# Third table parts on two halves of TensorE's rows, and stores of two rows each

## The reference

```
x_slice = take_along_axis(xf, DIMS[tile_idx])            # 16 of 1024 channels
u  = clip((x_slice - mn[tile]) / (mx[tile] - mn[tile] + 1e-8), 0, 1 - 1e-6)
gi = clip(int(u * 16), 0, 15);  x_local = (u - gi/16) * 16
delta = (spline_bases[tile, j, gi] + spline_slopes[tile, j, gi] * x_local) * output_scale[tile]
out = layernorm(x + (x + scatter(delta)))                # over 1024 channels
```

## Time and profile before

| what | value |
|---|---|
| time of the runs | 1272.38 us, median of 3 (1271.8 to 1273.63) |
| the profiled execution | 1269.53 us, its span 1267.8 us |
| start of the last stage | 1119 us |
| busy share of the span | PE 89%, DVE 86%, ACT 74%, POOL 65% |
| mean TensorE clock granted | 0.92; 0.5 of full speed throughout the last stage |
| read from DRAM, written | 69.06 MB, 101.04 MB |

### The profile page before, as it was taken

The page is one execution under the profiler, slowest core; times in us unless marked ns, Lnnn a source line. Parts: engine busy times, 40 slices in busy tenths (PEclk is TensorE's granted clock), DMA queues, the critical chain, the costliest instruction groups (busy, mean ns, idle before and its releaser), DMA issues. The chain is left out here.

```text
span 1267.8 us, 31481 instructions
## 1 busy us (share of the span) xinstructions
PE 1131.2 (89%) x9273; PEld 720.2 (57%) x9278; DVE 1085.1 (86%) x2538; ACT 943.7 (74%) x1805; POOL 818.3 (65%) x1647
## 2 busy tenths in 40 slices
PE   5799999999999999999999999999999996747620
PEld 4556666666666666666666666666666663511100
DVE  4888889898989898989898999989998978887873
ACT  4657888888888888888888888888888873524771
POOL 3125666676767676767676767676767666525565
PEclk9999999999999999999999999999999998755555
DMA  4112332322222222232222222222222223859998
GB/s 145 34 39 105 107 107 107 106 105 105 105 105 105 105 105 105 105 105 105 105 105 104 104 104 104 103 101 89 102 100 102 103 73 131 348 209 366 407 419 333
DMA packets 63474, 174.88 MB, mean 138 GB/s; under 512 B 11259, under 2 KB 22467, under 8 KB 63430
## 3 DMA queue, kind: packets, MB, share of 16 engines
q1 hardware_dynamic: 52118, 149.33, 31.8%
q10 hardware_dynamic: 5808, 23.07, 4.5%
q0 software_dynamic: 5504, 1.94, 1.1%
HBM read 69.06 MB, written 101.04 MB: 134 GB/s over the span
## 5 line engine op out<-in xcount | busy, mean ns | idle before, releaser
L1189 DVE SCALAR_TENSOR_TENSOR acc<-xT_all,cw_sb,acc 128x256 f32<-128x256 f32 x768 | 354.0, 520 | 6.5 <-ACT acc L848 6.5
L875 ACT ACTIVATE sg<-TS,bet,gam 128x256 f16<-128x256 f32 x244 | 123.6, 557 | 26.6 <-PE TS L493 26.4
L513 PE MATMUL PR<-xT_all,w_sb 128*128 128x256 f32 x512 | 138.7, 395 | 2.7 <-ACT xT_all L811 2.7
L525 PE MATMUL WKB<-w_sb,tS 128*128 128x512 f32 x256 | 137.3, 618 | 0.0
L848 ACT ACTIVATE acc<-xT_all,cb_sb,cw_sb 128x256 f32<-128x256 f32 x256 | 132.5, 592 | 4.2 <-DVE xT_all L1175 2.2
L595 PE MATMUL PR<-shT,w_mg_sb 128*64 128x128 f32 x2048 | 127.8, 278 | 6.5 <-ACT shT L857 6.5
L368 POOL TENSOR_TENSOR AT<-AT,Wm 128x128 f32<-128x128 f32 x210 | 108.3, 516 | 39.2 <-DVE AT L1215 24.4
L567 PE MATMUL OB<-th_all,AT 128*128 128x512 f32 x256 | 122.7, 602 | 5.9 <-DVE AT L368 2.0
L595 PE MATMUL PR<-shT,w_rk_sb 128*64 128x128 f32 x2048 | 125.9, 276 | 0.0
L595 PEld LDWEIGHTS PR<-shT,w_rk_sb 128*64 128x64 f32 x2048 | 110.5, 137 | 25.7 <-issue 25.7
L595 PEld LDWEIGHTS PR<-shT,w_mg_sb 128*64 128x64 f32 x2048 | 112.5, 138 | 18.9 <-issue 12.0
(11 more groups left out here) (274 smaller groups left out, 2773.8 us busy)
## 6 DMA issues: line engine op xcount, KB each, us to landing
xin_all<-in_x SPq DMA_DIRECT2D x32, 1024.0 KB
y_ring<-y_all SPq DMA_DIRECT2D x32, 1024.0 KB, 4.1
y_scratch<-y_all SPq DMA_DIRECT2D x32, 1024.0 KB, 6.1
own<-y_scratch SPq DMA_DIRECT2D x5, 2048.0 KB, 17.2
rows<-y_scratch SPq DMA_DIRECT2D x4, 2048.0 KB, 12.6
out<-rows ACTq DMA_DIRECT2D x4, 2048.0 KB, 18.6
out<-own ACTq DMA_DIRECT2D x3, 2048.0 KB, 20.5
RX<-RE SPq DMA_DIRECT2D x128, 32.2 KB
```

Source lines behind the costliest of these rows:

```text
L513: i = pe.matmul(PR[:, 0:T], w0_sb[:, blk, :], xT[b][:, blk, HIST:HIST + T], start=(blk == 0), stop=(blk == NB - 1))
L525: pe.matmul(WK[h][:], tS[b][:, chunk_cols(c)], w1_sb[:, half_cols(h)], start=True, stop=False)
L875: nc.scalar.activation(sg[:, blk, :], at[:, (blk % 2) * T:(blk % 2 + 1) * T], ACT.Sign, scale=gam[:, blk:blk + 1], bias=bet[:, blk:blk + 1 ...
L1189: v.scalar_tensor_tensor(acc[:, blk, :], xT[b][:, blk, i:i + T], cw_sb[:, blk, i:i + 1], acc[:, blk, :], ALU.mult, ALU.add).then_inc(e_con ...
```

## The change

Two edits. First, `t2s2` gets 128 partitions: the table part three stands in both halves. For a pair of columns the two 128-row matmuls come first, then the third part of column 0 on rows 0 to 63, and that of column 1 on rows 64 to 127. Second, in units 0 to 10 ScalarE issues a store after each two columns, with 1 MB, in place of one of 2 MB after four; the waits on p_st count 32 for such a unit.

```diff
-        t2s2 = sbw("t2s2", [NT, TC], BF16)
+        t2s2 = sbw("t2s2", [P, TC], BF16)
...
-                    link(v.tensor_copy(t2s2[:], t2i[0:NT, :]))
+                    link(v.tensor_copy(t2s2[:], t2i[:]))
...
+            def written(u):
+
+                return sum(32 if w < DIRECT else 16 for w in range(u % NS, u + 1, NS))
+
...
                 for u in range(NS, U - 1):
-                    sp.wait_ge(p_st[slot_id(u)], stored(u - NS))
+                    sp.wait_ge(p_st[slot_id(u)], written(u - NS))
                     load(u)
...
-                    pool.wait_ge(p_st[slot_id(u)], stored(u))
+                    pool.wait_ge(p_st[slot_id(u)], written(u))
...
                     pe.wait_ge(p_zf, s - 2)
+                    cols = [slice(j * HALF, (j + 1) * HALF) for j in range(2)]
                     for j in range(2):
-                        cols = slice(j * HALF, (j + 1) * HALF)
-                        pe.matmul(Z[s % 3][:, cols], ohT[:, 2 * s + j, :], t2s01[:], start=True, stop=False)
-                        i = pe.matmul(Z[s % 3][:, cols], ohT[0:NT, 2 * s + j, :], t2s2[:], start=False, stop=True)
+                        pe.matmul(Z[s % 3][:, cols[j]], ohT[:, 2 * s + j, :], t2s01[:], start=True, stop=False)
+                    for j in range(2):
+                        rows = slice(j * NT, (j + 1) * NT)
+                        i = pe.matmul(Z[s % 3][:, cols[j]], ohT[rows, 2 * s + j, :], t2s2[rows, :], start=False, stop=True)
                     i.then_inc(z_rd, 1)
...
-                        if u < DIRECT and n % 4 == 3:
+                        if u < DIRECT and n % 2 == 1:
+                            pair = slice(n % 4 - 1, n % 4 + 1)
                             act.wait_ge(p_row, n + 1)
-                            nc.scalar.dma_start(out_u[u], slot(u)).then_inc(p_st[slot_id(u)], 16)
+                            nc.scalar.dma_start(out_u[u][:, pair, :], slot(u)[:, pair, :]).then_inc(p_st[slot_id(u)], 16)
```

More of the change, by code:

```diff
@@ L733, in early_tables @@
                         for j in range(2):
-                            cols = slice(j * HALF, (j + 1) * HALF)
-                            pe.matmul(z[:, cols], ohT[:, 2 * t + j, :], t2s01[:], start=True, stop=False)
-                            i = pe.matmul(z[:, cols], ohT[0:NT, 2 * t + j, :], t2s2[:], start=False, stop=True)
+                            pe.matmul(z[:, half_cols(j)], ohT[:, 2 * t + j, :], t2s01[:], start=True, stop=False)
+                        for j in range(2):
+                            rows = slice(j * NT, (j + 1) * NT)
+                            i = pe.matmul(z[:, half_cols(j)], ohT[rows, 2 * t + j, :], t2s2[rows, :], start=False, stop=True)
                         i.then_inc(z_rd, 1)
@@ L1776, in _ @@
                 for u in range(U - 1):
-                    sp.wait_ge(p_st[slot_id(u)], stored(u))
+                    sp.wait_ge(p_st[slot_id(u)], written(u))
                 for n in range(4):
```

## The result

| | before | after |
|---|---|---|
| median | 1272.49 us (1267.02 to 1273.76, 9 runs) | 1265.57 us (1264.26 to 1268.87, 9 runs) |
| profiled execution, span | 1269.53, 1267.8 us | 1264.53, 1262.8 us |

The ratio is 0.9955, with a 95% interval of 0.994 to 0.997: 5.7 us faster (3.8 to 7.6). Forecast were 2.3 us, with 1267.5 as the lower end of the range. The direction was right, the size was not, and the time lies outside the range; a result clearly faster than no change had been given 0.40.

What follows compares the result with a forecast made beforehand. It took bytes and compute with scatters to end the last stage together; shortened by 2.1 and 4.8 us, the end moves 2.1, plus 0.2 for the last landing: 2.3, to 1270.1 us, range 1267.5 to 1273.0.

Steps and rivals of the forecast that it cites:

- Two paths end within 0.2 us: compute and scatters, and bytes: Last stage: last scatter lands at 1263.7, last store at 1263.5, so the gain is that of the path shortened less.
- Bytes -2.1, compute and scatters -4.8: the end moves by 2.1: Sum for the last stage: the smaller shortening counts, plus 0.2 for the last scatter's landing, 2.3 us in all.
- The page's chain: Profile's path back from the last scatter through VectorE, GpSimd and TensorE, by which the last stage hangs on compute.
- Bytes, -2.1: DMA transfers of the last stage: unit 0's earlier first store lets unit 8 load, and the bytes end, 2.1 us earlier.
- slower rival: The 22 stores of 1 MB move bytes more slowly: 1271.9 us, or a loss at 1274.5; chance 0.13.
- Table lookups, 0.48 a pair: TensorE's third parts overlap on row halves: 0.48 us saved a pair (bounds 0 to 0.54), 4.8 over VectorE's ten waits.
- Scatters land by 1258.9: GpSimd's last scatter is issued at 1253.3, 4.8 us earlier, and lands by 1258.9.
- ScalarE's breaks, cost 0: Eleven more store issues on ScalarE at 0.46 to 0.50 us, 5.3 in all, cost nothing on the path.
- Profiled execution and median: Whole kernel: profiled execution 1267.2 us and median 1270.1, taking the median as 2.85 above the profiled execution.
- Eight or nine in the last five slices: Reading of the page's DMA shares, in tenths, for the last stage; about two tenths for most of the span before.
- 1.02 without a break: Sign in the changed profile's last stage: the DMA share stays at 1.02 from 1147 on.
- the chain is right, the bytes follow: Rival for the last stage: bytes also shorten with everything issued earlier, the end moves 4.8 to 1267.6 us; chance 0.15.

Runs made afterwards that it cites:

- the lookups alone: Changed kernel with row halves for the third parts but whole 2 MB stores as before; ratio 0.9977 to the kernel before, 2.9 us faster.
- store of unit 0 only: Changed kernel with row halves, but only unit 0's store split in two, units 1 to 10 stored whole; ratio 0.995 to the kernel before.
- units 0 to 2 in halves: Changed kernel with unit 8 loaded in halves, DIRECT = 10 (four scatters fewer), and only units 0 to 2 stored in halves; ratio 0.9958 to the kernel before.

## Why the prediction was wrong

The step that failed is in its first part: "Two paths end within 0.2 us: compute and scatters, and bytes", with "the rest of the span is the end of the program". The two landings are within 0.2 us, but what stands behind them is not the same. Behind the stores' landing there are about 0.5 us (SyncE's last steps, and 0.2 to the end); behind the scatters' there are 4.1, of which 3.65 is a drain. The runs show the scatter path ending 3.8 us after the byte path before (SyncE's wait of 4.0, of which 0.2 is always there), a gain of 2.9 us by the lookups alone, which the prediction has at zero, and a drain of 43 ns once the scatters are gone. The sum "Bytes -2.1, compute and scatters -4.8: the end moves by 2.1" should have begun from two ends, bytes at 144.75 + 0.2 and scatters at 144.85 + 3.9 into the stage: then -2.1 and -4.8 give 142.9 and 143.9, and the end moves by 4.8. The page's chain, which names scatters, VectorE and TensorE and which the prediction set aside, was right about what ended the kernel before.

By its own steps:

- *Bytes, -2.1.* Right: the first store 2.28 earlier in the stage (forecast 2.33), the load of unit 8 2.03 (2.1), SyncE done 2.16 earlier. The last depends on the executions taken: SyncE is done at 143.84 to 144.85 in the three kernels with scatters that store unit 0 whole, and at 142.15 to 143.02 in the six that split it and load unit 8 whole, 2.1 apart in the mean. Splitting unit 0 alone gives all of it. The long stretch stayed at 409 GB/s. The slower rival falls: stores of 1 MB move at the old rate. The Trainium skill's table (DMA: Bandwidth & Descriptors, Bandwidth), 78% of peak for a load of 1 MB issued from GpSimd, does not carry over to these stores, which queue behind each other.
- *Table lookups, 0.48 a pair.* Mis-sized: 0.65, above its bound of 0.54. The term left out is that both weight loads of a row count are issued together, so a pair has two bare loads and not three; the overlap itself is 0.43, as line 570 had it. Ten waits fell by 7.1 us in all, the last scatter came 7.2 earlier in the stage (forecast 4.8), and the scatters' landing 6.2. With the third parts on the same rows, two changes of row count in a pair in place of four, the pair became 0.22 shorter. The Trainium skill (TensorEngine Tiling (Array Packing), Key Properties) says that a change of tiling mode drains the engine; the direction fits.
- *Scatters land by 1258.9.* At 1258.5, but by errors that cancel: the stage began 1.0 later, the last issue came 7.2 earlier in it, and the landing followed 6.7 after that issue in place of 5.6.
- *ScalarE's breaks, cost 0.* Right on the path, wrong in size: not 0.46 each but up to 2.5 for each half late in the stage (the earlier trace rows has one such issue of 2.63). Unit 11 was late and VectorE waited 2.3 us. That the queued stores covered it fits the kernel with the store of unit 0 only, which has no such wait and ends its stage within 0.5 us of this one.
- *Profiled execution and median.* The 2.85 us between them are no larger than the scatter between executions (the stage starts between 1117.4 and 1122.5); the profile after happens to start its stage 1.0 late, which hides part of the gain (5.0 in the spans, 5.96 in the stages).
- *"Eight or nine in the last five slices" of DMA share.* The last five digits of the earlier trace rows are 5, 9, 9, 9, 8; the 5 holds the first hole. Nothing in the sum hangs on it. The sign "1.02 without a break" would not have shown a full rate either, by the dips above.

The rival *the chain is right, the bytes follow* gave 1267.6, the nearest of the cases, but by another mechanism: the bytes did not follow; the bytes were never the last. After the change they are, with the drain 0.2 us ahead of them. What stays open is what the last store's landing waits for once the bulk of the bytes is through (the run with units 0 to 2 in halves).

## What to carry to other kernels

When two paths seem to end together, read each to the program's last instruction and not to its last landing: look for drains and final waits behind both. A wait of one engine at the end (here 4.0 us, put down to another engine's sequencer) is a question to be answered before any sum is made. And where executions differ by some us in a part that the change doesn't touch, measure from the start of the stage that it does.

## What the runs showed of the hardware

- GpSimd's drain at the program's end took 3.65 us behind 44 indirect DMAs of 128 x 64 B, 3.33 behind 40, 0.04 behind none: about 0.08 us for each.
- bf16 matmuls of 64 rows on the two row halves and into two halves of a PSUM tile run side by side at 1.2 GHz: 0.54 for both with their weights, where each took 0.54.
- A bf16 64-row matmul behind a 64-row one on the same rows, or a 128-row one behind a 128-row one, shows no bare weight load; one behind another row count does, 0.10 at 1.2 GHz (pairs of 2.15, 1.93 and 1.50 us with four, two and two such loads, the last with row halves).
- Late in the stage, with many stores outstanding, a ScalarE issue of 1 MB held the engine for 2.2 to 2.5 us, where it is 0.38 earlier; one of 2 MB held it for 2.6 (before) and 5.1 (store of unit 0 only).
- An indirect DMA issue on GpSimd takes 0.96 us, and 2.07 while VectorE runs its predicated copies on 1024 columns, but for the first one or two beside them (1.0 to 1.1).
- A DMA share of 0.99 went with 301 GB/s over 2 us of the kernel before, where the mean of the stretch is 410 at 1.02.
